# Interleaving the context matmuls with the score groups in the block-sparse attention phase of a fused transformer layer

## The reference

```python
q, k, v = heads(x @ Wq.T + bq), heads(x @ Wk.T + bk), heads(x @ Wv.T + bv)
first_ctx = attend(qb[:, :, 0], k, v)            # block 0 attends to all 64 blocks
second_ctx = attend(qb[:, :, 1], blocks 0, 1, 2, 63)
mid: query block i attends to blocks 0, i-1, i, i+1, 63
second_last_ctx = attend(qb[:, :, -2], blocks 0, 61, 62, 63)
last_ctx = attend(qb[:, :, -1], k, v)            # block 63 attends to all 64 blocks
x = x + layernorm(ctx)
x = x + layernorm(ffn(layernorm(x)))
```

## Time and profile before

| what | value |
|---|---|
| median of the timed runs | 2546.36 us (2 runs: 2458.72 and 2634.0) |
| the profiled execution, its time | 2466.82 us |
| its span, slowest core | 2465.2 us, so 1.6 us lie around it |
| spans of the 8 cores | 2440.8 to 2465.2 us |
| busy in the span | PE 1660.0 us, DVE 874.5, ACT 601.9, POOL 339.1 |

### The profile page before, as it was taken

How to read it: one execution, slowest core, us unless ns; L and a number is a source line. 1 busy time by engine, 2 the same in 40 slices (tenths; PEclk the granted TensorE clock), 3 DMA queues, 4 the chain that set the end, 5 groups by cost and what they waited for, 6 DMA issues and landing times.

```text
span 2465.2 us, 31515 instructions; the slowest of 8 cores (2440.8 to 2465.2 us)
## 1 busy us (share of the span) xinstructions
PE 1660.0 (67%) x11234; PEld 801.2 (32%) x11234; DVE 874.5 (35%) x2724; ACT 601.9 (24%) x794; POOL 339.1 (14%) x510
## 2 busy tenths in 40 slices
PE   0069999957777770000000799999998999999994
PEld 0034444434444440000000344444443444444442
DVE  3514343334344441477775111222323222323123
ACT  2411111155666440022222110211111111212121
POOL 1011212101111120000000111111120212111110
PEclk9999999967666775555555899999999999999997
DMA  9934233131111117966652953566585766665653
GB/s 224 270 86 79 76 66 84 39 112 62 53 53 65 47 29 138 197 153 138 148 146 109 113 56 34 60 116 65 111 77 103 73 116 61 115 61 92 86 66 103
DMA packets 359498, 239.34 MB, mean 97 GB/s; under 512 B 313008, under 2 KB 314672, under 8 KB 357296
## 3 DMA queue, kind: packets, MB, share of 16 engines
q0 software_dynamic: 225456, 111.33, 32.0%
q1 hardware_dynamic: 120064, 92.43, 15.4%
q10 hardware_dynamic: 13824, 33.56, 4.2%
HBM read 205.53 MB, written 75.63 MB: 114 GB/s over the span
## 4 chain that ended last, share of the span: by engine, by line
PE 41%; DMA 6%; DVE 6%; SPq 3%; ACT 2%; issue 1%; ACTq 1%; DVEq 0%; POOL 0%; POOLq 0%
PE gp L883 14%; PE upp L888 14%; PE yp L900 7%; DMA xn_d<-p_xn 5%; PE upp L900 3%; PE gp L900 3%; SPq L622 3%; DVE p_x L698 1%; ACT p_xn L768 1%; DVE y_sb L961 1%; DMA p_ctx<-ctxT_d 1%; DVE bst3b L704 1%; DVE p_attn L655 1%; DVE bst3b L706 1%; SPq L858 1%
## 5 line engine op out<-in xcount | busy, mean ns | idle before, releaser
L883 PE MATMUL gp<-x2T,wg_sb 128*128 128x512 bf16 x1536 | 375.7, 389 | 483.0 <-DMA x2T<-xn_d 446.8
L883 PEld LDWEIGHTS gp<-x2T,wg_sb 128*128 128x128 bf16 x1536 | 152.1, 99 | 673.6 <-issue 501.0
L888 PE MATMUL upp<-x2T,wu_sl 128*128 128x512 bf16 x1536 | 364.8, 380 | 0.0
L949 DVE TENSOR_TENSOR hswb<-upp,sgbuf 128x512 bf16<-128x512 f32 x192 | 132.8, 692 | 591.3 <-ACT sgbuf L927 591.3
L829 POOL DMA_DIRECT2D wu_sl<-wuT x192 | 168.1, 878 | 1036.6 <-PE upp L888 607.3
L525 ACT ACTIVATE arenaB<-psS 128x768 bf16<-128x768 f32 (+2 forms) x312 | 246.8, 850 | 150.7 <-PE psS L482 141.7
L927 ACT ACTIVATE sgbuf<-gp 128x512 bf16<-128x512 f32 x192 | 114.7, 597 | 570.5 <-PE upp L888 570.4
L482 PE MATMUL psS<-qt_buf,kt_buf 64*64 64x64 bf16 (+2 forms) x3232 | 163.6, 317 | 107.2 <-ACT arenaB L525 92.8
L888 PEld LDWEIGHTS upp<-x2T,wu_sl 128*128 128x128 bf16 x1536 | 151.3, 98 | 184.8 <-issue 6.5
L900 PE MATMUL yp<-wd_sb,hswb 128*128 128x512 bf16 x768 | 197.1, 379 | 14.0 <-DVE hswb L949 14.0
L375 PE MATMUL qp<-xn1T,wq_sb 128*128 128x512 bf16 x512 | 122.6, 383 | 123.4 <-DMA xn1T<-xn_d 123.4
(11 more groups left out here) (83 smaller groups left out, 1237.3 us busy)
## 6 DMA issues: line engine op xcount, KB each, us to landing
wu_sl<-wuT POOLq DMA_DIRECT2D x192, 256.0 KB, 4.9
xbuf<-x_in SPq DMA_DIRECT2D x32, 512.0 KB, 11.2
p_x<-x_in SPq DMA_DIRECT2D x32, 512.0 KB, 10.1
x_d<-p_x ACTq DMA_DIRECT2D x32, 512.0 KB, 6.8
x1f<-x_d SPq DMA_DIRECT2D x32, 512.0 KB, 5.0
out<-obuf POOLq DMA_DIRECT2D x32, 512.0 KB, 4.6
ctxT_d<-cstage POOLq DMA_DIRECT2D x128, 65.0 KB, 2.0
xn_d<-xn1buf ACTq DMA_DIRECT2D x32, 256.0 KB, 7.2
```

Source lines behind the costliest of these rows:

```text
L883: te.matmul(gsl, wg_sb[:, dc * FF + hc * 128:dc * FF + (hc + 1) * 128], x2T[:, par * 8 * 512 + dc * 512:par * 8 * 512 + (dc + 1) * 512], s ...
L888: mm = te.matmul(usl, wu_sl[:, (hc % 4) * 1024 + dc * 128: (hc % 4) * 1024 + (dc + 1) * 128], x2T[:, par * 8 * 512 + dc * 512:par * 8 * 51 ...
L949: v.tensor_tensor(hswb[:, hc * 512:(hc + 1) * 512], upp[:, (ghc % 2) * 512:(ghc % 2 + 1) * 512], sgbuf[:, (ghc % 2) * 512:(ghc % 2 + 1) * ...
```

## The change

The order of the work in a unit becomes a table, `P2_S_ORDER` with 39 positions: dense groups 1 to 6, then the 31 pair groups, then dense groups 0 and 7. `P2_CTX_ORDER` says after which position each chunk can run, which is the position of the last group that it reads: chunks 1 to 6 after positions 13, 17, 21, 25, 29 and 33, chunk 0 after 37, chunk 7 after 38. PE issues a chunk right behind the group at that position. `P2_CUM_MS` counts memset signals up to a position. ACT goes by the same table of groups; DVE and POOL go by both tables. No instruction is added or taken away; the buffers are the same, and those of a chunk now alternate by its place in the order.

```diff
+def _p2_sched():
+    s_order = [(0, gi) for gi in range(1, 7)]
+    s_order += [(t, None) for t in range(1, NP_)]
+    s_order += [(0, 0), (0, 7)]
...
+    for C in range(1, 7):
+        dep = pos_of[("p0", C)]
+        for (t, acol, pcol, w) in CTX_LISTS[C]:
+            if t > 0:
+                dep = max(dep, pos_of[("in", t)])
+        ctx_order.append((C, dep))
+    ctx_order.append((0, pos_of[("p0", 0)]))
+    ctx_order.append((7, pos_of[("p0", 7)]))
...
             def _(te):
                 for u in range(8):
...
-                    for gi in range(SGROUPS):
-                        gg = u * SGROUPS + gi
+                    oi = 0
+                    for p, (t, gi) in enumerate(P2_S_ORDER):
+                        gg = u * SGROUPS + p
                         if gg >= 2:
                             te.wait_ge(sm.s_exp, gg - 1)
...
                         last.then_inc(sm.s_spe, 1)
-                    te.wait_ge(sm.s_exp, SGROUPS * (u + 1))
-                    te.wait_ge(sm.s_ms, MS_INC_PER_U * (u + 1))
-                    for C in range(NCH):
-                        for h01 in (0, 1):
-                            if C >= 2:
-                                te.wait_ge(sm.s_cev0, 8 * u + C - 1)
-                                te.wait_ge(sm.s_cev1, 8 * u + C - 1)
+                        while oi < 8 and P2_CTX_ORDER[oi][1] == p:
+                            C, dep = P2_CTX_ORDER[oi]
+                            te.wait_ge(sm.s_exp, u * SGROUPS + dep + 1)
+                            te.wait_ge(sm.s_ms, u * MS_INC_PER_U + P2_CUM_MS[dep])
+                            if oi >= 2:
+                                te.wait_ge(sm.s_cev0, 8 * u + oi - 1)
+                                te.wait_ge(sm.s_cev1, 8 * u + oi - 1)
...
             def _(v):
...
+                        if t != 0 and MEMSETS[t]:
+                            v.wait_ge(sm.s_exp, gg + 1)
...
+                        while oi < 8 and P2_CTX_ORDER[oi][1] == p:
+                            v.wait_ge(sm.s_cpe, u * 16 + 2 * oi + 1)
```

More of the change, by code:

```diff
@@ L97 @@
 SGROUPS = 8 + (NP_ - 1)
+def _p2_sched():
+    s_order = [(0, gi) for gi in range(1, 7)]
+    s_order += [(t, None) for t in range(1, NP_)]
+    s_order += [(0, 0), (0, 7)]
+    pos_of = {}
+    for p, (t, gi) in enumerate(s_order):
+        if t == 0:
+            pos_of[("p0", gi)] = p
+        else:
+            pos_of[("in", t)] = p
+    ctx_order = []
+    for C in range(1, 7):
[6 more added lines that the diff above has]
+    ctx_order.append((7, pos_of[("p0", 7)]))
+    cum = []
+    acc = 0
+    for (t, gi) in s_order:
+        if t != 0 and MEMSETS[t]:
+            acc += 1
+        cum.append(acc)
+    return s_order, ctx_order, cum
+P2_S_ORDER, P2_CTX_ORDER, P2_CUM_MS = _p2_sched()
 MS_INC_PER_U = sum(1 for t in range(1, NP_) if MEMSETS[t])
@@ L463, in _ @@
                     te.wait_ge((sm.s_ql0, sm.s_ql1)[u % 2], 32 * (u // 2 + 1))
-                    if u >= 1:
-                        pass
-                    for gi in range(SGROUPS):
-                        gg = u * SGROUPS + gi
+                    oi = 0
+                    for p, (t, gi) in enumerate(P2_S_ORDER):
+                        gg = u * SGROUPS + p
                         if gg >= 2:
@@ L470, in _ @@
                         par = gg % 2
-                        t = 0 if gi < 8 else gi - 7
                         jt, jb = PAIRS[t]
@@ L500, in _ @@
                                 te.wait_ge(sm.s_cev1, 8 * u)
[L501 to L510, removed]
+                            for h01 in (0, 1):
+                                pc = (pc0, pc1)[h01]
+                                h = 2 * u + h01
+                                n_e = len(CTX_LISTS[C])
+                                for ei, (tt_, acol, pcol, w) in enumerate(CTX_LISTS[C]):
+                                    mm = te.matmul(
+                                        pc[0:65, (oi % 2) * 512 + pcol:(oi % 2) * 512 + pcol + w],
+                                        v_sb[:, tt_ * 1040 + h * 65: tt_ * 1040 + h * 65 + 65],
+                                        arenaB[:, h01 * A + acol:h01 * A + acol + w],
+                                        start=(ei == 0), stop=(ei == n_e - 1))
+                                mm.then_inc(sm.s_cpe, 1)
+                            oi += 1
+                    assert oi == 8
             @blk.scalar
@@ new lines, in _ @@
+                    for p, (t, gi) in enumerate(P2_S_ORDER):
+                        gg = u * SGROUPS + p
+                        if t != 0 and MEMSETS[t]:
+                            v.wait_ge(sm.s_exp, gg + 1)
+                            last = None
+                            for (half, lo, hi) in MEMSETS[t]:
+                                for h01 in (0, 1):
+                                    last = v.memset(
+                                        arenaB[half * 64:half * 64 + 64,
+                                               h01 * A + SEG_OFF[t] + lo:
+                                               h01 * A + SEG_OFF[t] + hi], 0.0)
+                            last.then_inc(sm.s_ms, 1)
+                        while oi < 8 and P2_CTX_ORDER[oi][1] == p:
+                            v.wait_ge(sm.s_cpe, u * 16 + 2 * oi + 1)
+                            if 4 * u + oi // 2 >= 1:
+                                v.wait_ge((sm.s_cs00, sm.s_cs01)[oi % 2], 16 * (4 * u + oi // 2))
+                            v.tensor_copy(cstage0[:, (oi % 2) * 512:(oi % 2 + 1) * 512],
+                                          pc0[0:65, (oi % 2) * 512:(oi % 2 + 1) * 512]).then_inc(sm.s_cev0, 1)
+                            v.wait_ge(sm.s_cpe, u * 16 + 2 * oi + 2)
+                            if 4 * u + oi // 2 >= 1:
+                                v.wait_ge((sm.s_cs10, sm.s_cs11)[oi % 2], 16 * (4 * u + oi // 2))
+                            v.tensor_copy(cstage1[:, (oi % 2) * 512:(oi % 2 + 1) * 512],
+                                          pc1[0:65, (oi % 2) * 512:(oi % 2 + 1) * 512]).then_inc(sm.s_cev1, 1)
+                            oi += 1
@@ L558, in _ @@
                 for u in range(8):
-                    for C in range(NCH):
-                        g.wait_ge(sm.s_cev0, 8 * u + C + 1)
+                    for oi, (C, dep) in enumerate(P2_CTX_ORDER):
+                        g.wait_ge(sm.s_cev0, 8 * u + oi + 1)
                         g.dma_start(ctxT_d[(2 * u) * 65:(2 * u) * 65 + 65,
                                            C * 512:(C + 1) * 512],
-                                    cstage0[:, (C % 2) * 512:(C % 2 + 1) * 512]).then_inc(
-                            (sm.s_cs00, sm.s_cs01)[C % 2], 16)
-                        g.wait_ge(sm.s_cev1, 8 * u + C + 1)
+                                    cstage0[:, (oi % 2) * 512:(oi % 2 + 1) * 512]).then_inc(
+                            (sm.s_cs00, sm.s_cs01)[oi % 2], 16)
+                        g.wait_ge(sm.s_cev1, 8 * u + oi + 1)
                         g.dma_start(ctxT_d[(2 * u + 1) * 65:(2 * u + 1) * 65 + 65,
                                            C * 512:(C + 1) * 512],
-                                    cstage1[:, (C % 2) * 512:(C % 2 + 1) * 512]).then_inc(
-                            (sm.s_cs10, sm.s_cs11)[C % 2], 16)
+                                    cstage1[:, (oi % 2) * 512:(oi % 2 + 1) * 512]).then_inc(
+                            (sm.s_cs10, sm.s_cs11)[oi % 2], 16)
     def _p3a():
```

## The result

The changed kernel is slower. Its runs have a median of 2606.73 us (2581.87 to 2758.58, 11 runs), those of the kernel before 2542.78 us (2458.72 to 2728.75, 10 runs). The ratio is 1.0549, interval 1.049 to 1.0607. The profiled execution took 2586.8 us against 2466.8, which is 120 us more.

The account below looks back on a forecast made before the run. The attention phase was taken as a strict sequence: a ring of exps and score groups, then PE alone. Gaps of 6 x 4.21 + 5.9 + 3.9 against 19.9 us gave 2466.8 + 122 = 2589 us, range 2535 to 2670.

Parts of the forecast that it names:

- the mechanism: In the attention phase, each chunk waits for its group's exp and holds back the next group, so ACT stops each time.
- the sum of 122 us: Gaps of ACT per unit rise from 19.9 to 35.1 us, +15.2 us, or +122 us for 8 units.
- The chain of a gap of chunks 1 to 6: Exp and memsets to chunk 0.92 us, chunk at lower clock 2.64, next group to its exp 0.65: 4.21 us.
- Chunks 0 and 7: ACT gaps at the unit's last two chunks: 5.9 us for chunk 0, 3.9 us for chunk 7.
- the 0.2 us from the exp to PE: Estimated delay from an exp's end to PE's start at chunks 0 and 7, about 0.2 us.
- 1.33 us for a small chunk at the upper clock: Time of each of chunks 1 to 6 on PE at the upper clock, against 2.64 us at the lower.
- The ring: Exp, score group, exp through the two halves of `psS`; restarting after each chunk costs under 0.1 us.
- The clock: PE's granted clock: lower level for chunks 1 to 6, upper for chunk 7; chunk 0 partly fast at 5.2 us.
- The rival with the clock up: Upper clock through the whole attention phase: +4.1 us per unit, +33 us, 2500 us; chance 0.10.
- The rival in which no rise comes: Chunks 0 and 7 both at the lower clock: +24 us in all, 2613 us; chance 0.10.
- the one in which the chunks are hidden: Chunks 1 to 6 run beneath the exps, leaving 9.8 us of gaps per unit: 2386 us; chance 0.03.
- an allowance at the upper end: Range reaches 2670 us in case the median again lies some 80 us above the profiled execution; otherwise 2565 to 2620.

Follow-up runs that it names:

- order_only: Changed kernel with the new order of groups, but all eight chunks issued after the unit's last group; ratio 0.9995 against the kernel before, median 2463.12 us.
- late1: Changed kernel with each chunk issued one group later, chunk 0 after position 38; ratio 1.0294 against the kernel before, median 2538.03 us.
- late2: Changed kernel with each chunk issued two groups later; ratio 1.0003 against the kernel before, median 2463.99 us.
- spread4b: Changed kernel with chunks cut into single matmuls, about 900 columns per group, three groups after release, casts before memsets; ratio 0.9473 against the kernel before, median 2332.97 us.
- filler: Changed kernel with unread 512-column matmuls on PE, one behind each pair group, four where a chunk follows; ratio 1.0214 against the kernel before, 2513.5 and 2514.5 us.
- nomemset: Changed kernel without the memsets and PE's wait for them; one run of 2564.5 us against the changed kernel's 2586.8.

## Why the prediction was right, and where it was wrong

*In short*: the mechanism held, and the sum of 122 us for the phase too, in part by luck. What failed is the base on which the sum was put: 2589 us was compared with a median that already lay 80 us above the execution from which 2589 was made.

*The mechanism* was right. The changed kernel puts each chunk behind the group that releases it, so the chunk is not hidden but gets a round trip of its own. order_only, late1 and late2 show it from one side, spread4b from the other.

*The chain of a gap of chunks 1 to 6*, 0.92 + 2.64 + 0.65 = 4.21 us, came out as 0.92 + 2.67 + 0.65 = 4.24. The first term is the memsets' end at 658.76 + 0.42 = 659.18 and the 0.36 us up to 659.54, behind an exp that ended at 655.51 + 3.11 = 658.62.

*Chunks 0 and 7* were too low: 6.42 and 4.28 us against 5.9 and 3.9. Two terms are at fault. The first is the 0.2 us from the exp to PE, taken from a score group. Ahead of chunk 7 it was 703.82 - (702.33 + 1.02) = 0.47 us, and 0.47 ahead of chunk 0 as well in seven of the eight units; the unit of the rows, with 696.36 - (694.71 + 1.02) = 0.63, is the exception. The exps of one instruction each show on ACT:

```profile
694.71 1.02 ACT L556 ACTIVATE arenaB<-psS 128x1024 bf16<-128x1024 f32 x1 [0.15 <-PE psS L511]
702.33 1.02 ACT L556 ACTIVATE arenaB<-psS 128x1024 bf16<-128x1024 f32 x1 [6.59 <-PE psS L511]
```

The second is the chunk itself. Chunk 0 took 5.40 us in the mean (4.50 to 5.92), put at 5.2, and chunk 7 3.27, put at 3.15. In the same way 1.33 us for a small chunk at the upper clock was too low: filler shows 1.40, as its matmuls are counted busy for 1.47 and the next group starts 0.07 before that ends.

Why a chunk starts later than a score group can be read from the first unit. A score group's first matmul has one semaphore to wait for, s_exp, and starts 0.14 us after the exp's end. A chunk's has s_exp, s_ms and the two of the casts. Only the first two chunks of the first unit have no casts to wait for; in later units the first two have, which the words on the kernel before left out. In nomemset such a chunk has s_exp alone and starts 521.96 - (516.21 + 5.61) = 0.14 us after the exp; with the two waits for casts it is 0.36.

```profile
516.21 5.61 ACT L555 ACTIVATE arenaB<-psS 128x768 bf16<-128x768 f32 x7 [0.19 <-PE psS L511]
```
```profile
521.96 2.74 PE L534 MATMUL pc<-arenaB,v_sb 128*65 128x512 bf16 x12 [1.06 <-ACT arenaB L555]
```

In the changed kernel the first chunk starts 517.14 - (516.57 + 0.42) = 0.15 us after its memsets, where chunks with the waits for casts take 0.36:

```profile
516.57 0.42 DVE L569 MEMSET arenaB<- 64x64 bf16 x4 [0.47 <-ACT arenaB L556]
```
```profile
517.14 2.74 PE L535 MATMUL pc<-arenaB,v_sb 128*65 128x512 bf16 x12 [1.63 <-DVE arenaB L569]
```

With three waits behind the one for the exp, at chunks 0 and 7, it is 0.47. So each wait that stands in the queue behind the one that ends last costs about 0.11 us, an estimate from these differences, although its own condition has long been met.

*The ring* went the other way: restarted from both halves of `psS`, four exps take 3.11 us and not 3.20, and a unit's exps 31.5 us and not 32.2. I had put under 0.1 us of cost on each restart, and it is under 0.1 us of gain. Gaps of 6 x 4.23 + 6.42 + 4.28 = 36.1 us less 19.9, less 0.7, are +15.5 us a unit. The forecast had +15.2. That it is so close is in part luck: chunks 0 and 7 were 0.9 us too low together, and the ring was 0.7 us too high.

*The clock* was right: 0.50 under chunks 1 to 6, a rise within chunk 0, 1.00 under chunk 7. Between chunks it did rise for moments, as the group of 0.36 us at 671.17 shows, and was down again at the next chunk. The rival with the clock up did not happen by itself. filler made it happen and got close to its place: 2513.5 where the rival had 2500, from the same 2.8 to 2.9 us per gap. The rival in which no rise comes, and the one in which the chunks are hidden, are out by the rows shown.

*The time* is where the prediction was wrong. The step that failed is "The profiled execution took 2466.8 us, so I get 2466.8 + 122 = 2589 us". The sum of +122 us was right: the two profiled executions differ by 120 and their phases by 124. But the kernel before stands in the table with a median of 2546.36, 80 us above that execution. Beside it 2589 forecasts 43 us, or 1.7%, where the measured ratio is 5.5% and the medians moved by 64 us, from 2542.78 to 2606.73. The text saw the 80 us and made them an allowance at the upper end in place of a part of the forecast, which was no better: the median after is only 20 us above its profiled execution. The effect should have been carried as a ratio, 122 / 2466.8 = 4.9%, with its own bounds. That is just inside the interval of the measured one, 4.9% to 6.1%.

## What to carry to other kernels

In-order queues overlap only what is issued ahead: a consumer that stands right behind the instruction that releases it adds a full round trip, and the producer's engine stops for as long as the consumer runs. Count for each moved piece how many units of work the other engine still has in hand when the wait begins. None cost 5.5% here, one cost 2.9%, two broke even, and three, with the pieces cut to fit the spare time of each group, gained 5.3%.

## What the hardware showed that was not expected

- Score groups with stops of only 0.2 to 0.5 us between them ran at the lower clock for 26.7 us on end. The Trainium skill ("TensorE: Matmul & The Clock Gate", section "Why this matters for your kernels") asks for short idle gaps to keep the clock. Here this was not enough, while the same groups with one filler matmul behind each ran with the phase at 0.89.
- Each further semaphore wait in front of a matmul cost about 0.11 us, even where its condition had long been met: from the end of the exp to the matmul 0.14 us with one wait (184 of 184 such score groups in the changed kernel, 285 of 286 in the kernel before), 0.36 with three (nomemset) and 0.47 with four (chunks 0 and 7). With two such waits behind the memsets at 48 chunks and three behind the exp at 16, that is about 48 x 0.22 + 16 x 0.33 = 16 us of the changed kernel, an estimate; a kernel without these waits was not run.
- spread4b has 258 us of PE work and 253 of ACT work within 308 us, and the kernel before 298 and 247 within 428. PE's same instructions count as busy for 40 us less, at a clock of 0.92 against 0.67. How much of it the clock alone makes is not shown: late2, at 0.71, is busy for 301.9 us, more than the kernel before, and a busy stretch of PE also counts the tail of its last matmul (1.47 us for a chunk of 1.40 in filler), so fewer stops make less busy time as well.
